# One low-rank product over two halves side by side, with W2, LoRA and W3 transfers and products in another order

## What is computed

```python
    x = x + _L0_cond_ref(x, L0_cond_weight, L0_cond_scale_log, condB_codebook, L0_cond_lora_A, L0_cond_lora_B)
    x = x + _L1_cond_ref(x, itok_B_0_7, L1_cond_W, L1_cond_Wr, L1_cond_A, L1_cond_B)
    x = x + _L2_cond_ref(x, itok_B_0_23, L2_cond_W, L2_cond_b, L2_cond_lora_As, L2_cond_lora_Bs)
    x = x + _L3_cond_ref(x, itok_B_0_15, L3_cond_weight)
```

## Time and profile before

| | us |
|---|---|
| median of 3 runs (689.34 to 691.33) | 689.86 |
| the profiled execution | 691.96 |
| its span | 690.1 |
| PE busy | 675.9 (98%) |
| DVE busy | 349.1 (51%) |
| ACT busy | 276.9 (40%) |
| POOL busy | 88.5 (13%) |

### The profile page before, as it was taken

One profiled execution on the slowest core, in us unless ns is written; L12 is line 12 of the kernel. 1 busy time (PEld: TensorE's weight loads), 2 busy tenths in 40 slices (PEclk: granted clock), 3 DMA queues, 4 the chain that ended last, 5 costly groups with the idle time before them and its releaser, 6 DMA issues.

```text
span 690.1 us, 9555 instructions
## 1 busy us (share of the span) xinstructions
PE 675.9 (98%) x3432; PEld 583.7 (85%) x3432; DVE 349.1 (51%) x532; ACT 276.9 (40%) x414; POOL 88.5 (13%) x128
## 2 busy tenths in 40 slices
PE   5899999999999999999999999999999999999998
PEld 5789999999999988788889878889888888888886
DVE  4799889879961364124543222661320653302353
ACT  5656473971813352123651022562121564012353
POOL 2200215005010021001211000311000111000020
PEclk9999999999999999999999999999999999999999
DMA  9932212001000107002874000777000576000263
GB/s 249 323 104 64 59 31 62 1 0 62 1 0 1 62 24 243 2 1 91 280 226 157 0 0 24 246 232 251 0 0 0 181 267 229 16 0 1 91 222 115
DMA packets 39331, 67.61 MB, mean 98 GB/s; under 512 B 3588, under 2 KB 23044, under 8 KB 39300
## 3 DMA queue, kind: packets, MB, share of 16 engines
q1 hardware_dynamic: 34976, 59.33, 27.0%
q10 hardware_dynamic: 4324, 7.87, 3.2%
HBM read 58.80 MB, written 8.39 MB: 97 GB/s over the span
## 4 chain that ended last, share of the span: by engine, by line
PE 92%; DMA 2%; SPq 2%; DVE 1%; issue 1%; ACT 1%; POOL 0%; DVEq 0%; ACTq 0%
PE ps L963 30%; PE ps L964 29%; PE ps L965 29%; DMA e_lo_w<-w_t 2%; PE ps L1082 1%; DMA raw<-w_t 1%; PE ps L976 1%; PE ps L1109 1%; PE ps L978 1%; SPq L399 0%; SPq L343 0%; ACT e_hi L590 0%; POOL e_lo_w L437 0%; SPq L331 0%; PE ps L1091 0%
## 5 line engine op out<-in xcount | busy, mean ns | idle before, releaser
L963 PE MATMUL ps<-e_hi,ring_hi 128*128 128x384 f32 (+3 forms) x384 | 135.0, 352 | 7.8 <-DVE e_lo L702 7.7
L702 DVE TENSOR_TENSOR ring_lo<-raw,ring_hi 128x512 fp32r<-128x512 f32 x128 | 91.0, 725 | 92.1 <-ACT ring_hi L614 92.1
L965 PE MATMUL ps<-e_hi,ring_lo 128*128 128x384 f32 (+3 forms) x384 | 134.6, 351 | 0.0
L614 ACT ACTIVATE ring_hi<-raw 128x512 fp32r<-128x512 f32 x128 | 79.5, 629 | 79.8 <-PE ps L965 61.4
L963 PE MATMUL ps<-x_both,e_hi 128*128 128x512 f32 x256 | 101.8, 398 | 0.0
L964 PE MATMUL ps<-x_both,e_hi 128*128 128x512 f32 x256 | 101.2, 395 | 0.0
L965 PE MATMUL ps<-x_both,e_lo 128*128 128x512 f32 x256 | 100.7, 393 | 0.0
L963 PE MATMUL ps<-ring_hi,e_mid 128*128 128x512 f32 x256 | 99.6, 389 | 0.0
L964 PE MATMUL ps<-ring_lo,e_mid 128*128 128x512 f32 x256 | 99.6, 389 | 0.0
L965 PE MATMUL ps<-ring_hi,e_mid 128*128 128x512 f32 x256 | 99.6, 389 | 0.0
L963 PEld LDWEIGHTS ps<-e_hi,ring_hi 128*128 128x128 f32 x384 | 73.3, 191 | 14.0 <-DVE e_lo L702 8.3
(11 more groups left out here) (143 smaller groups left out, 906.2 us busy)
## 6 DMA issues: line engine op xcount, KB each, us to landing
raw<-w_t SPq DMA_DIRECT2D x64, 512.0 KB, 4.1
xraw<-x_t SPq DMA_DIRECT2D x16, 512.0 KB, 4.6
w_w<-w SPq DMA_DIRECT2D x15, 512.0 KB, 5.1
y<-tmp ACTq DMA_DIRECT2D x30, 256.0 KB, 4.1
e_lo_w<-w_t SPq DMA_DIRECT2D x4, 512.0 KB, 10.9
e_lo_w<-w_t SPq DMA_DIRECT2D x4, 384.0 KB, 5.7
e_mid_w<-bs SPq DMA_DIRECT2D x24, 64.0 KB, 2.4
w_w<-w SPq DMA_DIRECT2D x2, 256.0 KB, 4.0
```

The costliest lines, as they stand in the source:

```text
L614: act.activation(ring_hi[:, (2 * k + h) % 4, :], raw[:, k % RAW, h * 512:(h + 1) * 512], ACT.Copy).then_inc(w3_hi, 1)
L702: return dve.tensor_tensor(out, whole, hi.bitcast(F32), ALU.subtract)
L963: pe.matmul(out, a[0], b_[0], start=start, stop=False, **kw)
L965: return pe.matmul(out, a[1], b_[0], start=False, stop=stop, **kw)
```

## The change

Three edits, and what they need.

1. The high and the low half of E become one tile `e_both`, so that one matmul can read the same columns of both. Low_rank issues two matmuls per contraction step and token tile in place of three: x's high part against both halves (2 x 152 columns, into one bank), and x's low part against the high half (152 columns, onto the first 152). A token tile has a bank of its own, four banks (4 to 7) in all. A batch's 152 columns are its own 16 adapter columns and the 136 shared ones: the second batch's adapter columns are copied ahead of the shared ones, the first one's behind them. ACT copies the second 152 columns of each bank to `tok`, DVE adds the first 152; the gate, the transposes and the adapter columns then read `tok`. `turn_h2` goes ahead of `turn_g`, into bank 5, and `h2_add` adds onto its result, with the small matrix as the stationary operand.
2. W2's second part is requested ahead of LoRA's matrices, and split ahead of them; `lora(0..3)` go behind chunk 2. W0's first two tiles are requested ahead of the adapters A. POOL clears LoRA's padding in DVE's place. W1's first half goes to ACT's queue.
3. In a group, W3's first four tiles are requested ahead of b and x.

The core of the diff (renamed semaphores, the new views of buffers and DVE's new operands are left out):

```diff
-EW = EC + 2 * R2
-TW = ER + NE + 2 * R2
+EW = EC + R2
+TW = ER + NE + R2
+SLOT = [7 if i == 1 else 3 + i // 2 if i % 2 else i // 2 for i in range(NB)]
+TILE_AT = [A0, A0 - R2]
+A_AT, WR_AT, NOW_AT = [0, R2], [ER, R2 + ER], [ER + NE, 0]
...
-    plan += [("w2", 0, kk) for kk in W2_ORDER[0][2:]] + [("bcat",), ("w1", 1), ("lora",), ("f", 0), ("br", 0)]
-    plan += [("w2", 1, kk) for kk in range(3)] + deltas(0, 1) + [("w2", 1, 3), ("f", 1)] + deltas(2, 3)
-    plan += [("thr",), ("as",)] + [("w2", 2, kk) for kk in range(4)] + [("f", 2)] + some(3)
-    plan += [("br", 1)] + some(3) + [("f", 3)] + deltas(4) + [("w1", 2)] + some(1) + [("f", 4)] + some(1)
-    plan += deltas(5) + [("br", 2), ("f", 5)]
+    plan += [("w2", 0, kk) for kk in W2_ORDER[0][2:]] + [("bcat",), ("w1", 1), ("f", 0)]
+    plan += [("w2", 1, 0), ("w2", 1, 1), ("br", 0), ("w2", 1, 2), ("w2", 1, 3), ("lora",), ("f", 1), ("thr",)]
+    plan += [("f", 2)] + deltas(0, 1, 2, 3) + [("as",)] + [("w2", 2, kk) for kk in range(4)] + some(2)
+    plan += [("br", 1)] + some(2) + [("f", 3)] + some(1) + deltas(4) + some(1) + [("w1", 2), ("f", 4)] + some(1)
+    plan += deltas(5) + some(1) + [("br", 2), ("f", 5)]
...
+        e_hi, e_lo = e_both[:, 0, :, :], e_both[:, 1, :, :]
+        e_mid = mid[:, 0:KT * EC].rearrange("p (k c) -> p k c", c=EC)
+        e_mid_w = mid_w[:, 0:KT * EC].rearrange("p (k c) -> p k c", c=EC)
+        scl, rscl = scales[:, 0, :, :], scales[:, 1, :, :]
...
+        tok = mid_w[:, 8704:8704 + 4 * TW].rearrange("p (t c) -> p t c", t=4)
+        bs_raw = mid_w[0:96, 8704 + 4 * TW:9728 + 4 * TW]
+        h2_tok = scales[:, :, :, :].rearrange("p a k e -> p (a k e)").rearrange("p (t c) -> p t c", t=4)
...
-            for half, signal in ((1, s_w1_first), (0, s_w1[0])):
-                sp.dma_start(w1_raw(0)[:, 4 * half:4 * half + 4, :],
-                             w1[half * 512:(half + 1) * 512, 0:P].rearrange("(k p) c -> p k c", p=P)).then_inc(signal, 16)
-                for kk in W2_ORDER[0][:2] if half else W2_ORDER[0][2:]:
-                    load_w2(0, kk)
+            for kk in W2_ORDER[0][:2]:
+                load_w2(0, kk)
+            sp.dma_start(w1_raw(0)[:, 0:4, :], w1[0:512, 0:P].rearrange("(k p) c -> p k c", p=P)).then_inc(s_w1[0], 16)
+            for kk in W2_ORDER[0][2:]:
+                load_w2(0, kk)
             sp.dma_start(bcat_raw, bcat.rearrange("p (k t) -> p k t", t=P)).then_inc(s_bcat, 16)
             load_w1(1)
+            for kk in range(4):
+                load_w2(1, kk)
...
-            for kk in range(4):
-                load_w2(1, kk)
+            load_w0(0)
+            load_w0(1)
...
             def group(g, last):
+                for k in range(RAW):
+                    load_w3(g, 0, k)
                 load_bs(g)
                 if not last:
                     load_x(g + 1, 0)
                     load_x(g + 1, 1)
-                for k in range(KT):
+                for k in range(RAW, KT):
                     load_w3(g, 0, k)
...
+                elif item[0] == "lora":
+                    pool.wait_ge(lora_hi, 2)
+                    pool.memset(stack_al[R0:P, :].bitcast(F32), 0.0).then_inc(lora_clear, 1)
+                    pool.wait_ge(lora_clear, 1)
...
-            def now(g):
-                pool.wait_ge(h2_mm, g)
+            def now(g, first):
+                pool.wait_ge(h2t_mm, g)
                 for j in range(2):
-                    cols, at_col = bass.ds(U0 + R2 * j + 2 * R2 * g, R2), EC + R2 * j
-                    pool.tensor_copy(e_hi[:, :, at_col:at_col + R2], e_hi[:, :, cols]).then_inc(now_ready, 1)
-                    pool.tensor_copy(e_lo[:, :, at_col:at_col + R2], e_lo[:, :, cols]).then_inc(now_ready, 1)
-                    pool.tensor_copy(br_now_hi[:, j, :], br_hi[:, cols]).then_inc(now_ready, 1)
-                    pool.tensor_copy(br_now_lo[:, j, :], br_lo[:, cols]).then_inc(now_ready, 1)
+                    if j == 0:
+                        cols, to = bass.ds(U0 + R2 * g, R2), EC
+                    else:
+                        cols, to = slice(A0 - R2, A0) if first else bass.ds(U0 + 3 * R2 + R2 * g, R2), A0 - R2
+                    if j == 1 and first:
+                        pool.sem_inc(now_ready, 1)
+                    else:
+                        pool.tensor_copy(e_both[:, :, :, to:to + R2], e_both[:, :, :, cols]).then_inc(now_ready, 1)
+                    own = slice(R2 * j, R2 * (j + 1))
+                    pool.tensor_copy(br_now_hi[:, j, own], br_hi[:, cols]).then_inc(now_ready, 1)
+                    pool.tensor_copy(br_now_lo[:, j, own], br_lo[:, cols]).then_inc(now_ready, 1)
...
+            act.dma_start(w1_raw(0)[:, 4:KT, :], w1[512:D, 0:P].rearrange("(k p) c -> p k c", p=P)).then_inc(s_w1_first, 16)
...
+                act.wait_ge(t_done, g + 1)
+                act.activation(tok, ps[:, 4:8, TW:2 * TW], ACT.Copy).then_inc(part_done, 1)
+                act.wait_ge(tok_done, g + 1)
+                act.wait_ge(h2_clear, 1)
+                for j in range(2):
+                    act.activation(h2_tok[:, 2 * j:2 * j + 2, R2 * j:R2 * (j + 1)],
+                                   tok[:, 2 * j:2 * j + 2, NOW_AT[j]:NOW_AT[j] + R2], ACT.Copy).then_inc(h2_tok_done, 1)
...
-                dve.wait_ge(t_done, g + 1)
+                dve.wait_ge(part_done, g + 1)
+                dve.tensor_tensor(tok, ps[:, 4:8, 0:TW], tok, ALU.add).then_inc(tok_done, 1)
+                dve.wait_ge(tok_done, g + 1)
...
+                if n == 2:
+                    pe.wait_ge(lora_lo, 2)
+                    pe.wait_ge(lora_clear, 1)
+                    for u in range(4):
+                        lora(u)
                 if n in BR_AFTER:
                     br(BR_AFTER[n])
-                if n == 1:
-                    pe.wait_ge(lora_lo, 3)
-                    for u in range(4):
-                        lora(u)
...
             def low_rank(g):
-                pe.wait_ge(now_ready, 8 * (g + 1))
-                pe.wait_ge(y_free, KT * g + 4)
+                pe.wait_ge(now_ready, 6 * (g + 1))
+                pe.wait_ge(y_free, KT * g + 8)
                 for k in range(KT):
                     for t in range(4):
-                        j = t // 2
-                        rhs = (e_hi[:, k, A0:EW], e_lo[:, k, A0:EW])
-                        cols = slice(t * P, (t + 1) * P)
-                        ins = product(ps[:, 5 + j, (t % 2) * TW:(t % 2 + 1) * TW],
-                                      (x_hi[:, k, cols], x_lo[:, k, cols]), rhs,
-                                      k == 0 and t % 2 == 0, k == KT - 1, skip_group_check=True)
+                        cols, ecols = slice(t * P, (t + 1) * P), slice(TILE_AT[t // 2], TILE_AT[t // 2] + TW)
+                        pe.matmul(ps[:, 4 + t, 0:2 * TW].rearrange("p (h c) -> p h c", h=2), x_hi[:, k, cols],
+                                  e_both[:, :, k, ecols], start=k == 0, stop=False, skip_group_check=True)
+                        ins = pe.matmul(ps[:, 4 + t, 0:TW], x_lo[:, k, cols], e_hi[:, k, ecols],
+                                        start=False, stop=k == KT - 1, skip_group_check=True)
                 ins.then_inc(t_done, 1)
...
             def h2_add(g):
-                pe.wait_ge(gt_done, g + 1)
-                for t in range(4):
-                    j = t // 2
-                    c0 = (t % 2) * TW + ER + NE + R2 * j
-                    cols = slice(t * P, (t + 1) * P)
-                    ins = product(ps[:, 5 + j, c0:c0 + R2], (gt_hi[:, cols], gt_lo[:, cols]),
-                                  (br_now_hi[:, j, :], br_now_lo[:, j, :]), False, True, skip_group_check=True)
-                ins.then_inc(h2_mm, 1)
             def turn_h2(g):
                 pe.wait_ge(h2_tok_done, 2 * (g + 1))
                 for t in range(4):
-                    ins = pe.matmul(ps[0:32, 7, t * P:(t + 1) * P], h2_tok[:, t, :], ident[:, :],
-                                    start=True, stop=True)
+                    pe.matmul(ps[0:32, 5, t * P:(t + 1) * P], h2_tok[:, t, :], ident[:, :],
+                              start=t == 0, stop=False, skip_group_check=True)
+            def turn_g(g):
+                pe.wait_ge(g_done, 4 * (g + 1))
+                for t in range(4):
+                    at = A_AT[t // 2]
+                    ins = pe.transpose(ps[:, 7, t * P:(t + 1) * P], tok[:, t, at:at + ER], ident[:, :])
+                ins.then_inc(gt_mm, 1)
+            def h2_add(g):
+                pe.wait_ge(gt_done, g + 1)
+                for j in range(2):
+                    cols = slice(2 * j * P, 2 * (j + 1) * P)
+                    ins = product(ps[0:32, 5, cols], (br_now_hi[:, j, :], br_now_lo[:, j, :]),
+                                  (gt_hi[:, cols], gt_lo[:, cols]), False, True, skip_group_check=True)
                 ins.then_inc(h2t_mm, 1)
...
                 low_rank(g)
                 x3_main(g, 1)
                 x3_main(g, 2)
+                turn_h2(g)
```

(37 more changed lines are left out.)

41 lines of the change are left out of this document (12 added, 29 removed).

## The result

The changed kernel takes 678.74 us (median of 4 runs, 677.79 to 679.95) against 689.6 for the kernel before on the same chip; the ratio is 0.9835, with a 95% interval of 0.9818 to 0.9853. It is faster by some 11 us, where 17.8 were forecast, and lies above the range of 667.5 to 676.0. The profiled execution took 679.95 us with a span of 678.1.

The account below looks back on a forecast made before the run. PE's own queue was taken as the bound. Savings of 10.7 + 2.2 + 0.6 + 4.0 + 0.3 = 17.8 us bring the profiled 691.96 to 674.2; less 2.1 for the median, 672.1 us, 8-in-10 range 667.5 to 676.

Parts of the forecast that it names:

- The low-rank product: PE's 32 pairs a group: two matmuls at 0.250 us a pair replace three at 0.334, 8.0 us a group, 10.7 saved.
- The line and the floor: PE's matmul price between starts: 0.45 ns a column, but at least 0.111 us each, paid below some 240 columns.
- (a): Low-rank product: stationary operands load further ahead, a pair costs two floors, 0.222 us; 668.5 us in all, chance 0.10.
- (c): Low-rank product: the wide two-run matmul costs two floors, 0.222 us, so nothing is saved there; 682.8 us, chance 0.05.
- (d): Low-rank product: the two-run operand streams slower, 0.278 us at twice the time per column; kernel slower, chance 0.03.
- h2_add: PE's h2 products: 6 matmuls of 256 columns replace 12 of 16, 1.26 to 0.71 us a group, 2.2 saved.
- The exchange on ACT and DVE: ACT's copy and DVE's addition ahead of the gate take 1.9 us of 4.9 us of cover; cost nothing.
- W3 first: First group's gate: W3 tiles land earlier, so PE's wait at the gate's products goes; 0.6 us saved (0 to 0.8).
- W2 ahead of LoRA: First phase: PE's 2.6 us wait and slow clock shrink, stretch 23.05 to 19.1 us; 4.0 saved (2 to 4.4).
- As, w0 and W2's third part cost nothing: First phase: moving these loads on SP costs nothing, since PE wants W2's third part only at 42 us.
- (b): First phase: PE, now earlier, meets DVE's chain at 52 us or POOL's additions, 1 to 3 us stalled; 674 us, chance 0.12.
- The start: Before the first matmul: W1's first half on ACT's queue takes 0.3 us (0 to 0.5) off PE's 7.7 us wait.

Follow-up runs that it names:

- best: The changed kernel with 128 bytes per partition more behind the third part and W0's first two tiles requested behind the adapters and W2's third part; 673.33 us.
- adapters_first: The changed kernel with W0's first two tiles requested behind the adapters A and W2's third part again; 677.58 us.
- pad128: The changed kernel with 128 bytes per partition more behind the third part, moving x, the rings and everything behind them; 674.77 us.
- before_pad128: The kernel before with 128 unused bytes per partition between the third part and x; 693.33 us against 690.03.
- shift_both: The changed kernel with 128 unused bytes ahead of the third part, moving x3 and the rings together; 192 y products in 44.62 us.
- pad64: The changed kernel with 64 bytes more behind the third part; 192 y products in 44.80 us.
- pad256: The changed kernel with 256 bytes more behind the third part; 192 y products in 44.62 us.
- best_rows: The version best with e_both's rows 8 floats longer, 5248 bytes from one k to the next instead of 5216; 672.25 us against 673.33.
- best_w3_late: The version best with W3's first four tiles requested behind b and x, as before the change; 677.71 us.

## Why the prediction was right or wrong

**The low-rank product: right.** 8.00 us a group, 10.7 saved. The line and the floor read from the earlier trace rows priced a size that no row showed, and the two-run operand cost nothing extra: rivals (a), (c) and (d) fall. The Trainium skill ("TensorE: Matmul & The Clock Gate", on the array as 16 sub-arrays) has PE's queue pull weight loads ahead; if it did so here, it didn't bring a pair to 0.222. The starts at 0.139 and 0.111 did not show: 0.18 and 0.07, with the forecast sum.

**h2_add: right.** 0.70 us against 0.71. The 32-wide stationary operand costs nothing.

**The exchange on ACT and DVE: right in the changed kernel, for a reason the prediction missed.** PE doesn't wait for the gate. But the cover of 4.9 us was read in the third group; in the first, ACT's copy stands behind the W3 splits, and only the third part of the change clears them.

**W3 first: the size may hold, its role was missed.** 0.6 us were counted for the wait that went. Alone it is at most about that; beside the new copy it keeps 4.4 us from being lost. What failed here is the reading of the queue: the prediction saw the splits hold DVE until 270.6 and didn't ask what the first part adds behind them on ACT.

**W2 ahead of LoRA: right mechanism, mis-sized term.** The new stretch came out as worked out (23.05 us became 19.1, from 22.89 to 42.01). Its worth is 2.5 us between medians and not 4.0. The profiled execution, 2.1 above the median in the prediction's figures, was one with a stall of 2.6 and a fall of the clock; for such runs 4.0 is nearly right (about 3.8), but more than half of the old kernel's runs (22 of 39) are at full clock and gain about 1.8. The prediction took those 2.1 us off the result and counted the same stall as gain: the excess went in twice.

**"As, w0 and W2's third part cost nothing": wrong.** The failed step is that this order was dismissed by asking when PE wants W2's third part (42 us), and not when DVE wants it and the adapters. The quantisation's first step on DVE came at 37.40 and not by 35.2 (1.4 ahead of 36.58), and ring_lo ended 1.26 us later than before in place of 1.4 earlier. With the loads in the old order the prediction's reckoning of DVE comes out: that step 1.1 to 1.7 us earlier than before ("best" and adapters_first), no wait at 52. The stall itself is rival (b)'s, at 1.2 us of the median.

**The placement: put at nothing without a reason.** This is the largest failed step. The edit lengthens a tile by 128 bytes, the prediction costed no layout and took the y products as unchanged; they cost 1.06 us more in each group, 4.0 of the median (678.74 to 674.77). Its last sentence expects, above 676 with the low-rank product as forecast, a wait or a fall of the clock that it had not named. It is neither: the same matmuls at full clock, further apart.

**The start: wrong by 0.3.** Nothing measurable.

The ledger from the runs: 10.7 + 2.2 from the two traces, 2.5 for W2 ahead, 0 to 0.6 for W3, less 4.0 for the placement and 1.2 for the adapters, is 10.2 to 10.8, against 10.9 measured between the medians. With the last two taken back, "best" gains 17.0 us, 690.33 to 673.33, against 15.4 to 16.0 by the same ledger. Some 0.5 of the rest stands in the groups' traces: from group to group "best" is 3.4 us shorter, of which the low-rank product and h2_add make 3.25. In the second group the x3 tile behind h2_add (5.76 to 5.58) and the closing products behind it (4.82 to 4.62) have become shorter, other stages a little longer. Why wasn't tested, and the remaining 0.5 to 1 us has no name.

## What to carry to other kernels

Price short matmuls from the distance between starts at neighbouring sizes; it held to 0.01 us. If the profiled execution lies above the median, find its excess before you count it as gain: it is a stall that the other runs don't have. For each step that is moved, ask who on every engine wants it and what else the same change queues behind it, and write down the new addresses of all tiles behind one whose size changes, since 128 bytes moved 4 us.

## What the hardware showed that was not expected

A 512-column matmul of the y products costs 0.2268 to 0.2270 us from start to start when x3 and the rings lie a multiple of 256 bytes apart, and 0.2323 to 0.2333 at the other distances tried (128 and 192 modulo 256), at full granted clock, with no wait shown (the kernel before and pad128 fast; the changed kernel, before_pad128, shift_both, pad64 and pad256 slow). No other pair of tiles was shown to follow this: the x3 products (best_rows) didn't. The printed mean duration moves with it, 389 ns against 394 or 395, so it can be found in the table of matmuls by line. The same row of that table (busy us, mean ns of one) in pad128 and in the changed kernel:

```profile
L992 PE MATMUL ps<-ring_hi,e_mid 128*128 128x512 f32 x256 | 99.7, 389 | 0.0
```
```profile
L992 PE MATMUL ps<-ring_hi,e_mid 128*128 128x512 f32 x256 | 101.0, 395 | 0.0
```

A wait of 2.05 us at 271 us was followed by a granted clock of 0.75 from 275 to 280, which is part of the stretch at 1.2 GHz and the rest at 2.4, and one of 1.4 to 1.9 us at 26 or 54 us by none (1.00) in the profiles: the cost of a wait can be almost double its length. Whether the clock falls also differs from run to run of one kernel: nine of the old kernel's 17 runs above had a mean clock of 0.999 or more and eight had less, 2 us longer. Where it fell in these isn't seen, but all 41 runs of the kernels with W2 ahead of LoRA have 0.999 or more, best_w3_late aside, so it is most likely the wait for LoRA's eviction.
